# One transformer-like layer pair on one core: the gate's silu as one ScalarE activation

## What is computed

```python
x  = L0_attn_hidden_states                      # (2, 512, 256)
xn = layernorm(x)
s  = attention(xn)                              # 16 heads of 16, 4 chosen blocks of 32 keys
g  = silu(ffn(xn))
x  = x + s * g

def ffn(x):                                     # 8 experts, 2 per token, hidden width 176
    scores = softmax(x @ gate_w)
    topk_w, topk_idx = top_k(scores, 2)
    comb = scatter(topk_w at topk_idx)
    g = silu(einsum('td,edh->teh', x, w_gate)) * einsum('td,edh->teh', x, w_up)
    routed = einsum('teh,ehd,te->td', g, w_down, comb)
    shared = silu(x @ sw_gate) * (x @ sw_up) @ sw_down      # width 352
    return routed + shared
```

## Time and profile before

| | us |
|---|---|
| median of 3 timed runs | 406.1 |
| lowest and highest of them | 405.85, 408.53 |
| the profiled execution | 409.56 |
| its span in the trace | 407.7 |

### The profile page before, as it was taken

The page is one execution under the profiler, slowest core; times in us unless marked ns, Lnnn a source line. Parts: engine busy times, 40 slices in busy tenths (PEclk is TensorE's granted clock), DMA queues, the critical chain, the costliest instruction groups (busy, mean ns, idle before and its releaser), DMA issues. The chain is left out here.

```text
span 407.7 us, 5771 instructions
## 1 busy us (share of the span) xinstructions
PE 313.8 (77%) x1762; PEld 203.5 (50%) x1762; DVE 279.1 (68%) x865; ACT 164.7 (40%) x332; POOL 122.7 (30%) x105
## 2 busy tenths in 40 slices
PE   0699638567578799899899999994625998995981
PEld 0487527455344455555555555542614784444741
DVE  3857799986489778777234444447839969378694
ACT  1413611451012223232665656562303676938510
POOL 2555545577002111111113434445145000000123
PEclk9999897988588899999999999999685898998898
DMA  8992377456998374755443424015017000000011
GB/s 276 307 287 62 103 166 213 128 149 229 247 183 175 105 178 115 207 161 149 111 143 93 127 77 118 0 29 181 0 33 240 0 2 0 0 0 2 0 51 51
DMA packets 52545, 47.88 MB, mean 117 GB/s; under 512 B 5282, under 2 KB 50204, under 8 KB 52509
## 3 DMA queue, kind: packets, MB, share of 16 engines
q1 hardware_dynamic: 50211, 42.12, 38.7%
q0 software_dynamic: 1872, 4.22, 3.0%
q10 hardware_dynamic: 432, 1.18, 1.0%
HBM read 35.44 MB, written 15.87 MB: 126 GB/s over the span
## 5 line engine op out<-in xcount | busy, mean ns | idle before, releaser
L501 POOL DMA_INDIRECT yt_dram<-ysb,x x23 | 23.0, 1001 | 117.5 <-ACT ysb L617 78.9
L673 ACT ACTIVATE PT<-bank 128x512 f32<-128x512 f32 (+1 forms) x88 | 44.9, 559 | 21.5 <-PE bank L1177 20.8
L889 DVE TENSOR_REDUCE mx<-bank 128x1 f32<-128x384 f32 (+3 forms) x88 | 52.2, 636 | 1.5 <-PE bank L1159 0.8
L1158 PE MATMUL bank<-KS,QS 112*128 112x128 bf16 (+3 forms) x128 | 34.9, 319 | 12.3 <-DVE mx L889 10.7
L1788 PE MATMUL lbank<-u,w_ai 128*128 128x512 f32 x72 | 33.0, 619 | 1.9 <-issue 1.9
L1176 PE MATMUL bank<-QS,KS 115*128 115x512 bf16 (+3 forms) x128 | 31.0, 302 | 2.7 <-ACT PT L673 1.1
L1491 POOL TENSOR_TENSOR left<-xn,x 128x256 f32<-128x256 f32 x8 | 6.9, 897 | 85.9 <-DVE xn L1718 85.9
L1032 DVE SCALAR_TENSOR_TENSOR s<-th,bank 128x176 f32<-128x176 f32 x23 | 7.7, 336 | 33.7 <-ACT th L705 33.6
L507 POOL TENSOR_TENSOR small<-small,mhalf 128x16 f32<-128x16 f32 x8 | 24.4, 3046 | 17.3 <-DVE small L935 17.3
L1158 PEld LDWEIGHTS bank<-KS,QS 112*128 112x128 bf16 x128 | 12.7, 100 | 31.0 <-DVE mx L889 26.5
L1159 PE MATMUL bank<-tri,ident_b 128*128 128x128 bf16 x128 | 25.6, 227 | 0.0
(11 more groups left out here) (280 smaller groups left out, 807.8 us busy)
## 6 DMA issues: line engine op xcount, KB each, us to landing
wr<-w_dram SPq DMA_DIRECT2D x12, 352.0 KB
wt<-w_dram SPq DMA_DIRECT2D x11, 352.0 KB
QS<-parts_dram SPq DMA_DIRECT2D x12, 256.0 KB
KS<-parts_dram SPq DMA_DIRECT2D x12, 256.0 KB, 5.2
xs_dram<-x SPq DMA_DIRECT2D x1, 2967.0 KB, 15.4
x<-xs_dram SPq DMA_DIRECT2D x23, 129.0 KB, 2.8
w_dram<-in_w_chunks_dram SPq DMA_DIRECT2D x11, 256.0 KB, 4.8
wr<-in_w_chunks_dram SPq DMA_DIRECT2D x12, 176.0 KB
```

The costliest lines, as they stand in the source:

```text
L501: pool.indirect_dma_start(yt_dram, bass.IndirectOffsetOnAxis(ap=xg[:, n % XBUF, D:D + 1].bitcast(I32), axis=0), ysb[:, n % 2, :], None, bo ...
L673: act.activation(PT[:, k % 8, 0:n], bank[k % 2][:, 0:n], ACT.Exp, scale=float(DH) ** -0.5).then_inc(P_ready, 1)
L889: dve.tensor_reduce(mx[:, b * TB + i, heads[0]:heads[-1] + 1], bank[k % 2][:, 0:len(heads) * n].rearrange("p (h n) -> p h n", n=n), AX.X, ...
L1158: pe.matmul(out, QS[0:R_MAX, b, h, i * P:(i + 1) * P], KS[0:R_MAX, b, h, 0:n], start=True, stop=False)
```

## The change

In the six shared steps and in the tiles of steps 6 to 19 ScalarE computes silu(G) itself, and VectorE multiplies it by U. The `s2` operation, with the wait between it and `gb`, is gone there. Tiles of steps 20 to 28 keep tanh. The reader of bank 3 in the shared steps is now ScalarE alone, so `gate_product` waits for `th_ready` in place of `G_read`; `th` is read by `gb`, so ScalarE's next activation waits for `g_ready`.

```diff
             for s in range(SHARED):
                 act.wait_ge(G_ready, s + 1)
                 if s >= 1:
-                    act.wait_ge(G_read, s)
-                act.activation(th[:, :], bank[3][:, :], ACT.Tanh, scale=0.5).then_inc(th_ready, 1)
+                    act.wait_ge(g_ready, s)
+                act.activation(th[:, :], bank[3][:, :], ACT.Silu).then_inc(th_ready, 1)
...
                 act.wait_ge(G_ready, SHARED + i + 1)
-                if i:
-                    act.wait_ge(g_ready, SHARED + i)
+                act.wait_ge(g_ready, SHARED + i)
+                if s < DVE_STEP:
+                    act.activation(th[:, 0:EH], bank[3][:, 0:EH], ACT.Silu).then_inc(th_ready, 1)
                 else:
-                    act.wait_ge(G_read, SHARED)
-                act.activation(th[:, 0:EH], bank[3][:, 0:EH], ACT.Tanh, scale=0.5).then_inc(th_ready, 1)
+                    act.activation(th[:, 0:EH], bank[3][:, 0:EH], ACT.Tanh, scale=0.5).then_inc(th_ready, 1)
...
             for s in range(SHARED):
-                dve.wait_ge(th_ready, s + 1)
-                if s >= 1:
-                    dve.wait_ge(g_ready, s)
-                dve.scalar_tensor_tensor(out=s2[:, :], in0=th[:, :], scalar=1.0, in1=bank[3][:, :],
-                                         op0=ALU.add, op1=ALU.mult).then_inc(G_read, 1)
                 qs = step_slots(s)
                 slot(qs[0])
                 dve.wait_ge(U_ready, s + 1)
-                dve.wait_ge(G_read, s + 1)
+                dve.wait_ge(th_ready, s + 1)
                 if s >= 1:
                     dve.wait_ge(gh_ready, s)
                     dve.wait_ge(gl_ready, s)
-                dve.scalar_tensor_tensor(out=gb[:, :], in0=s2[:, :], scalar=0.5, in1=bank[4][:, :],
-                                         op0=ALU.mult, op1=ALU.mult).then_inc(g_ready, 1)
+                dve.tensor_tensor(gb[:, :], th[:, :], bank[4][:, :], ALU.mult).then_inc(g_ready, 1)
...
                 dve.wait_ge(th_ready, SHARED + i + 1)
-                link(dve.scalar_tensor_tensor(out=s2[:, 0:EH], in0=th[:, 0:EH], scalar=1.0, in1=bank[3][:, 0:EH],
-                                              op0=ALU.add, op1=ALU.mult))
+                if s >= DVE_STEP:
+                    link(dve.scalar_tensor_tensor(out=s2[:, 0:EH], in0=th[:, 0:EH], scalar=1.0, in1=bank[3][:, 0:EH],
+                                                  op0=ALU.add, op1=ALU.mult))
...
+                if s < DVE_STEP:
+                    dve.tensor_tensor(tile_gb(i), th[:, 0:EH], bank[3][:, EH:GU], ALU.mult).then_inc(g_ready, 1)
+                else:
...
                 pe.wait_ge(wl_ready, w + 1)
                 if s >= 1:
-                    pe.wait_ge(G_read, s)
+                    pe.wait_ge(th_ready, s)
```

More of the change, by code:

```diff
@@ L305, in layer0 @@
         wh_ready, wl_ready = m.sem("wh_ready"), m.sem("wl_ready")
-        G_ready, U_ready, th_ready, G_read, g_ready, gh_ready, gl_ready, down_done = (
-            m.sem(n) for n in ("G_ready", "U_ready", "th_ready", "G_read", "g_ready", "gh_ready", "gl_ready",
+        G_ready, U_ready, th_ready, g_ready, gh_ready, gl_ready, down_done = (
+            m.sem(n) for n in ("G_ready", "U_ready", "th_ready", "g_ready", "gh_ready", "gl_ready",
                                "down_done"))
@@ L1038, in _ @@
                     dve.wait_ge(U_ready, SHARED + i - 1)
-                dve.scalar_tensor_tensor(out=tile_gb(i), in0=s2[:, 0:EH], scalar=0.5, in1=bank[3][:, EH:GU],
-                                         op0=ALU.mult, op1=ALU.mult).then_inc(g_ready, 1)
+                if s < DVE_STEP:
+                    dve.tensor_tensor(tile_gb(i), th[:, 0:EH], bank[3][:, EH:GU], ALU.mult).then_inc(g_ready, 1)
+                else:
+                    dve.scalar_tensor_tensor(out=tile_gb(i), in0=s2[:, 0:EH], scalar=0.5, in1=bank[3][:, EH:GU],
+                                             op0=ALU.mult, op1=ALU.mult).then_inc(g_ready, 1)
                 slot(qs[0])
```

## The result

The changed kernel takes 403.38 us (median of 20 executions, 399.95 to 407.46), the kernel before beside it 406.06 us (20 executions, 404.05 to 409.79). The ratio is 0.9938, 95% interval 0.9915 to 0.9962: 0.6% or 2.5 us faster. (Every ratio here leaves out the executions that took over 1.5% longer than the fastest of the same kernel, so it can differ a little from the quotient of the medians.) The forecast was 400.2 us, 5.9 us faster.

What follows compares the result with a forecast made beforehand. VectorE was taken to bound the shared steps, a loop through TensorE and VectorE the first pass, TensorE the second. -1.9 (start) - 5.2 (tiles) + 1.2 (second load) = -5.9 us from 406.1 gave 400.2 us, range 398.2 to 405.0.

Steps and rivals of the forecast that it cites:

- hidden, cost 0: First table load, before the first silu: its 1.30 us delay fits ahead of TensorE's product at 46.84 and costs nothing.
- the three `s` operations: Second to fourth `s` on VectorE in the shared steps: removal saves 0.77 + 0.60 + 0.60 us before the bias copy.
- TensorE's wait in the shared steps: Next gate product waits for `th` instead of `s`, filling 4.89 us of idling; counted at nothing, other end 4.6 us.
- the price of two operands in SBUF: Kept multiplication: the 1.33 us product at 48.97 taken as its dearer end; the forecast stayed with cost 0.
- The second table load: Before the second pass's first exponential: waits for the same scores and delays TensorE, +1.2 us, ends 1.3 and 0.6.
- a lower clock: Sign of being wrong: TensorE's clock lower where it now idles longer in the shared steps; no size given.
- The tile steps: Tiles 0 to 13 lose `s`, 0.37 us each: 5.2 us saved, lower bound 2.8.
- rival 3: TensorE's order holds the tile steps, which save only 2.8 us: 402.6 us; chance 0.08.
- rival 4: Transfers pace the tile start and steps, leaving only the exposed load: slower, 407.3 us; chance 0.07.
- The start of the tiles: Shared steps: less VectorE work before the bias moves the expert tiles 1.9 us earlier, bounds 1.4 and 2.0.
- Rival 1: The tile start doesn't move because rows and scattered transfers set it, not SyncE's list: 402.1 us; chance 0.15.
- Rival 2: Each table switch costs a drain, making the second load 2.6 us: 401.6 us; chance 0.10.

Runs made afterwards that it cites:

- the overlap gone: Changed kernel with the silu table loaded right behind the router's exponential and the cast of weight chunk 1 behind it: 404.25 us against 409.04, ratio 0.9895.
- the kernel with the load placed: Changed kernel with a one-column exponential behind the last gate silu, loading the second table early: 403.73 us against 407.66, ratio 0.9895; also part of later combined runs.
- the loads alone: Kernel before plus a one-column silu behind the router's exponential, bringing both table loads with the old arithmetic: 412.27 us against 409.04, ratio 1.0091.
- the filled wait: Changed kernel with four unread score products in TensorE's wait behind the second table load: 407.29 us, ratio 0.9935 to the kernel before.
- the runs with the placed first load: Changed kernel with silu table and chunk 1 cast early: alone 0.9895; second load also placed 0.9876; with bias rows behind tile 7 0.999, behind tile 6 0.9831.
- the bias rows behind tile 7: Changed kernel with both table loads placed and the second batch's bias rows moved from behind tile 5 to tile 7: 408.38 us, ratio 0.999 to the kernel before.
- Behind tile 6: Changed kernel with both table loads placed and the second batch's bias rows moved from behind tile 5 to tile 6: 401.49 us against 409.12, ratio 0.9831.

## Why the prediction was right and where it wasn't

*The step that failed: "43.96 + 1.30 = 45.26: hidden, cost 0", for the first load.* I took its delay along the chain load, cast, split, TensorE's product at 46.84, and that chain has room. The delay bites elsewhere: GpSimd's split, moved later against VectorE's chain, holds `pl<-rpick` or the cast behind it until it ends. The distance from the exponential to the mask cast went from 4.72 to 5.98 us (+1.26), and since TensorE's transposes then ran at the lower clock (0.54 us more) the next copy of X came 1.80 us later. From there to the bias copy the three `s` operations gave back 1.80 - 0.06 = 1.74 us, near the 1.97 that I had worked out: gain and loss cancelled. Each alone shows its size: +1.66 us with the loads and the old arithmetic, and -2.02 us against before with the new arithmetic and the overlap gone (0.26 of it because `pl<-rpick` is held less than it was before, 1.76 for the `s`; TensorE's wait in the shared steps, counted at nothing in the sum, adds nothing that shows).

The profile of before had the sign: a TENSOR_SCALAR of 64 columns at 0.56 us where its neighbours take 0.2, ending 0.05 us behind GpSimd's operation. It had more of them:

```profile
37.94 1.28 POOL L523 TENSOR_TENSOR qkr<-rot_a,rot_b 128x512 f32<-128x512 f32 x1 [0.84 <-DVE rot_b L763]
...
38.02 1.28 DVE L816 TENSOR_TENSOR rt<-lg,rm 128x64 f32<-128x64 f32 x1
```

This product of 64 columns takes 1.28 us, ends 0.08 us behind GpSimd's, and stands directly ahead of the router's exponential; a like one without GpSimd (`sc<-rt,rm`, 41.20) takes 0.23. And the product at 48.97 in the earlier trace rows, 1.33 us long, was read in the prediction as the price of two operands in SBUF, though the same operation at 79.53 in the same rows takes 0.68: at 48.97 a GpSimd operation had been running since 48.47 and ended at 49.74. The Trainium skill has the rule, in "SBUF — State Buffer", section "Who interferes with whom": VectorE and GpSimd share a pair of ports that is locked for a whole instruction; copy, cast and tensor_scalar in their two-port modes can contend for it, and an instruction with at most one SBUF input outside them doesn't. The traces agree: TENSOR_SCALAR (1.82 and 1.83) and CAST (1.69) were held, MAX8 (0.69 for eight) wasn't.

*The second table load: sized at 1.2, measured at 1.2 or at 2.6 to 2.8.* Place and mechanism were right: it waits for the scores and delays the exponentials, and TensorE's fourth group goes later. Where the clock stayed at 1.00 the step took 6.87 us, 1.22 above the 5.65 of the kernel with the load placed. Where it fell to 0.50 (from 190.9 to 194.3 us in the changed kernel's profile) the step took 8.20 to 8.46, another 1.3 to 1.6 us. Of the eight profiled executions with this load left in its place (the loads alone and the filled wait among them) it fell in four. I had named a lower clock as a risk only for the shared steps (where it came too, as shown above), and not where the load makes TensorE wait. That the wait brings the fall is the best guess, as it never fell in the four profiles with the load placed, nor before; but four of eight against none of five is too few to show it, and that filling the wait prevents the fall isn't shown either.

*The tile steps: 14 x 0.37 = 5.2, of which 13 lie between tile 0 and tile 13 (4.8); measured 3.55.* The nine steps from tile 4 to 13 gave 0.36 each, as worked out, and the unit costs (0.32 for silu, 0.34 for the product) were exact. From tile 3 to 4 the gain was 0.03: there TensorE also transposes the bias and was busy 4.93 of 5.17 us before, with only 0.24 us to give, so its order holds the step. I had written that VectorE is full throughout the tiles with selection work; it was busy 9.05 of 9.55 us from tile 0 to 1 and 6.15 of 6.49 from 1 to 2, but 7.02 of 9.34 from 2 to 3, so that sentence was wrong for one of the three. From tile 0 to 3 the gain was 0.27 instead of 1.1, with 2.2 us of waiting for the weights of tile 2 where it had been 0.7. So rival 3 holds for one step, and rival 4 at least in part for three; the granted clock differs there too (from tile 2 to 3 0.82 before and 0.99 after), and the two can't be told apart. How much rival 4 takes varies: those three steps took 23.6 to 25.1 us in the eleven profiled executions with the change in the tiles, and 24.2 in the kernel with the loads alone, whose tiles are the old ones. What share of their gain the transfers and the clock take stays open.

*The start of the tiles.* From bias copy to the first tile's rows copied took 28.62 us before and 26.8 to 29.0 in the other executions, without a trend. So the 1.07 us in the second row of the table can't be told from this scatter; the 2 us of the runs with the placed first load came through to their sums. Rival 1 (the start doesn't move) comes nearest, but for another reason than it gave: the bias was ready no earlier, so SyncE's list never moved (asked for at 82.40 before and 81.57 after, 43.07 and 43.13 us behind the exponential). That TensorE took the first rows at 107.4, as forecast, is luck: 0.9 us of it lie ahead of the exponential, where nothing was changed.

*Rival 2, a drain with each switch, falls,* although its 2.6 us look like the 2.55 of the changed kernel's profile: where the clock held, the same load behind the same wait cost 1.22 us (6.87 - 5.65 in three profiles, 7.24 - 6.02 in the loads alone). The first load starts 0.01 us after the activation ahead (38.44 + 0.26 = 38.70, load at 38.71), and behind the second the activation follows 0.02 us after (190.44, 190.46). The Trainium skill, in "ScalarE: Activation LUTs", section "What ACT_TABLE_LOAD costs", states 1.38 us more; no load of these runs shows it.

In sum: forecast -5.88. The first load took the whole 1.9 of the shared steps, of which 1.0 came back within the scatter of the start, so 0.9 is missing there; 1.2 is missing in tiles 0 to 4 and 1.35 at the second load, by the clock in that profile. That leaves -2.33 by the stages. The -2.5 of the ratio is near it, but that the two agree is in part chance: each profile lies some 4 us from its median.

## What to carry to other kernels

A delay handed to another engine is not paid only by those who wait for its result. Where it moves an operation of GpSimd or VectorE, look also at what runs on the other of the two, and take a short operation with an odd length (0.56 where its kind takes 0.20) that ends with one of the other engine as held by it: the hold moves when either queue moves. A table load that comes with the first activation inherits that activation's waits; one column of the same function, behind the last activation of the old set, puts it into idle time and was worth 1.2 to 2.8 us in the profiles here. When an edit is added to two that work, time it alone: one constant took 4.5 us in one step and covered both.

## What was unexpected of the hardware

- A VectorE operation of 8 columns took 1.82 us instead of 0.16 while a GpSimd operation ran, and one issued 0.07 us ahead of GpSimd took its usual 0.19.
- The same program, with the same wait of 0.94 us on TensorE, had a granted clock of 1.00 behind it in one execution and of 0.72 and 0.50 in the next two stretches of 2 us in another.
- A transfer's place in SyncE's list can cost microseconds: with the bias rows behind tile 7 the two steps from tile 5 to 7 took together 14.6 us. Behind tile 6 they took 10.1, but behind tile 5 anything from 10.1 (the changed kernel) to 12.6 (the filled wait), so only the loss is shown.
